# An audio block with experts on one core: TensorE signals per group instead of per matmul

## The chip, the cores and the metric

The kernel runs on one core of a Trainium2 chip. The metric is the device time of one execution in microseconds. A core has TensorE (matmuls and transposes), VectorE, ScalarE, GpSimd and SyncE, each with its own instruction stream; they wait for each other by semaphores, which an instruction raises when it is done. TensorE has a granted clock with two levels, 1.2 and 2.4 GHz.

## The reference

`x` is 64 x 125 x 128. Three steps, the second and third on a layernorm and added to their input:

```
conv = conv1d(x, kernel, window 3)                 # -> 64 x 123 x 384, cut in Z, F, O
c_t  = sigmoid(F) * c_{t-1} + (1 - sigmoid(F)) * tanh(Z);   h = sigmoid(O) * c_t
h    = h + gelu(long_conv(layernorm(h), filters from A, B) + h0 * layernorm(h))
logits = layernorm(h) @ gate.T;  top 2 of 16 experts per token;  weights = softmax(top values)
hid  = silu(x @ w1[e].T)                            # 512 wide, for each token's experts
mean = (sum of hid over the tokens of e) / count;   y[e] = mean @ w2[e].T
h    = h + weights[k] * y[expert k of the token], summed over k
```

So the experts need only the sum of `silu(x @ w1[e].T)` over the tokens routed to each expert.

## The kernel before, in words

The whole program is written out by hand, one function per engine; the order in each is the order of the calls there. Its parts in time: the recurrence over 16 chunks (to 127 us), the long convolution as Toeplitz matmuls (133 to 160), layernorm and logits, then the routing (178 to 244), the expert stage (248 to 403), the sums and the mix (to the end).

**Routing.** It goes in four parts of 16 sequences (`q` = 0 to 3, the first `QA` = 2 of them make a first list of tiles). For each part: `ranks` counts, `places` (VectorE) takes the place of each token in its expert's list, `bit_transposes` and `matches` make 16 of the 32 one-hot matrices on TensorE, four matmuls into two PSUM banks in turn, each read by one ScalarE activation (`low_onehots`, line 1164); VectorE makes the other 16. `picks` is 32 small matmuls, each with a signal on `pick_mm`; ScalarE copies their result (`copy_V`, line 1151), and `pick_transposes` turns it. The lists of token indices that result are what GpSimd gathers by.

**Expert stage.** `NT` = 138 tiles of 128 tokens, each tile for one expert. GpSimd gathers a tile from a table in HBM (line 586); the first 48 tiles have places of their own, the others go through a ring of 12 (four groups of three). Tiles stand in 45 groups of three and three groups of one. TensorE, for each group `g`: transposes of group `g + 1` into one bank (line 872), then the three experts of group `g` (line 898, 128 x 512, fp32, two matmul records a tile), each into one of six banks. ScalarE copies the transposed group to one of two buffers (line 1202) and does the Silu of each tile in place (line 1210). VectorE adds the bank to the sum of that tile's expert (line 1612). Which expert a tile has is read from SBUF into registers, six tiles at a time, by a load in TensorE's and in VectorE's stream (lines 888 and 1604), ahead of tiles 6, 12, 18 and so on. After tiles 23 and 26 TensorE also turns the routing weights (line 974), which VectorE makes between tiles 15 and 18 (lines 1688 and 1690), ScalarE copies (line 1238) and VectorE splits (line 1697). Tiles 0 to 47 are written out, 48 to 131 are a loop of twelve, the last six are written out.

The waits there: TensorE's transposes of group `g` wait for their gathers and for the copy of group `g - 1`; tile `n` waits for the addition of tile `n - 6`. ScalarE's copy of group `g` waits for its transposes and for the experts of group `g - 2`; the Silu of tile `n` waits for that tile (`expert_mm`). GpSimd gathers ring group `g` when the transposes of group `g - 4` are done (the first one that waits is group 20, for group 16).

Of the kernel before, what the change touches and what calls it, by code (L numbers as in the profile page):

```python
# [40 lines left out]
QB = 16  # L41
# [80 lines left out]
def build(nc, x, wconv, fa, fb, h0, gate, w1, w2, dft, idft, route, match, out, kpad, table):  # L122
# [11 lines left out]
    with ctx:  # L134
# [244 lines left out]
        g_transposed = sem("g_transposed")  # L379
        GT_ready = sem("GT_ready")  # L380
        expert_mm = sem("expert_mm")
# [47 lines left out]
        def _(sp):  # L429
# [77 lines left out]
            sp.wait_ge(g_transposed, EARLY_GROUPS)  # L507
# [8 lines left out]
        def _(pool):  # L516
# [97 lines left out]
        def _(pe):  # L614
# [113 lines left out]
            def picks(q):  # L728

                pe.wait_ge(OHc_ready, q + 1)  # L730
                for n in range(2 * QB):
                    if n >= ON_ACT:
                        pe.wait_ge(onehot, q * ((2 * QB - ON_ACT) // OB) + (n - ON_ACT) // OB + 1)
                    else:
                        pe.wait_ge(ring_read, MATCH_AT[q, n // OG] + 1)
                    b, k = n // 2, n % 2
                    nc.tensor.matmul(P[q][:, QW + b * E:QW + (b + 1) * E], ohl[q % 2][0:T, n],
                                     OHc[0:T, q % 2, k * QW + b * E:k * QW + (b + 1) * E], start=(k == 0),
                                     stop=(k == 1)).then_inc(pick_mm, 1)
# [7 lines left out]
            def matches(q):  # L747
                pe.wait_ge(bitsT_ready, q + 1)
                for a in range(PER_Q):
                    at = MATCH_AT[q, a]  # L750
                    pe.wait_ge(ring_read, at - 1)
                    part = slice(a * OG * BITS, (a + 1) * OG * BITS)
                    nc.tensor.matmul(PR[at % 2][0:T, :], bitsT[part, :], matchb[part, :],  # L753
                                     start=True, stop=True).then_inc(ring_mm, 1)
# [111 lines left out]
            def g_transposes(g, landed, sources):  # L866
# [6 lines left out]
                mm.then_inc(g_transposed, 1)  # L873
# [16 lines left out]
            def expert(n, bank, stat, k):  # L890
# [5 lines left out]
                elif n == 5:  # L896
                    pe.wait_ge(idx_ready, 2)
                nc.tensor.matmul(bank[:, :], stat, w1T[:, bass.ds(e * FF, FF)],  # L898
                                 start=True, stop=True).then_inc(expert_mm, 1)

            def expert_of(n):
# [8 lines left out]
                expert(n, expert_bank(n), GTs[:, g % 2, j * SLOT:(j + 1) * SLOT], n)  # L910
# [66 lines left out]
            with pe.Fori(UNROLLED // UNROLL, NT // UNROLL) as i:  # L977
                for j in range(UNROLL // GG):
# [7 lines left out]
                    for k in range(GG):  # L986
                        expert(i * UNROLL + j * GG + k, XP[(j * GG + k) % len(XP)],
                               GTs[:, j % 2, k * SLOT:(k + 1) * SLOT], j * GG + k)
# [46 lines left out]
        def _(act):  # L1035
# [102 lines left out]
            def code_OH(q):  # L1138
# [3 lines left out]
                if q >= 2:  # L1142
                    act.wait_ge(pick_mm, 2 * QB * (q - 1))
# [3 lines left out]
            def copy_V(q):  # L1147
                act.wait_ge(pick_mm, 2 * QB * (q + 1))
# [10 lines left out]
            def low_onehots(q):  # L1159
                for a in range(PER_Q):  # L1160
                    act.wait_ge(ring_mm, MATCH_AT[q, a] + 1)
                    if q >= 2:
                        act.wait_ge(pick_mm, 2 * QB * (q - 2) + (a + 1) * OG)
# [33 lines left out]
            def copy_GT(g, bank, done, count=GG):  # L1197

                act.wait_ge(g_transposed, g + 1)
                if done is not None:  # L1200
                    act.wait_ge(expert_mm, done)
                nc.scalar.copy(GTs[:, bank, 0:count * SLOT], PT[:, 0:count * SLOT]).then_inc(GT_ready, 1)  # L1202

            def copy_of(g):
                if g < len(GROUPS):
                    copy_GT(g, g % 2, sum(GROUPS[g - 2]) if g >= 2 else None, GROUPS[g][1])

            def silu(n, bank):
                act.wait_ge(expert_mm, n + 1)
                nc.scalar.activation(bank[:, :], bank[:, :], ACT.Silu).then_inc(silu_done, 1)  # L1210

            def silu_of(n):
                silu(n, expert_bank(n))
# [17 lines left out]
            for n in range(UNROLLED):  # L1231
                if n % GG == 0:
                    copy_of(n // GG + 1)
                silu_of(n)
                if n in RT_AT:
                    h = RT_AT.index(n)
                    act.wait_ge(RT_mm, h + 1)
                    nc.scalar.copy(xh[:, h, 0:4 * T], PRT[:, 0:4 * T]).then_inc(RT_high, 1)
            with act.Fori(UNROLLED // UNROLL, NT // UNROLL) as i:
                for j in range(UNROLL // GG):  # L1240
                    g = i * (UNROLL // GG) + j
                    copy_GT(g + 1, (j + 1) % 2, i * UNROLL + j * GG)
                    for k in range(GG):
                        silu(i * UNROLL + j * GG + k, XP[(j * GG + k) % len(XP)])
            for n in range(NT // UNROLL * UNROLL, NT):
                g = next(i for i, (first, count) in enumerate(GROUPS) if first <= n < first + count)
                if n == GROUPS[g][0]:
                    copy_of(g + 1)
                silu_of(n)
# [18 lines left out]
        def _(dve):  # L1268
# [235 lines left out]
            def low_onehots(q, part):  # L1504
                n = slice(ON_ACT + part * OB, ON_ACT + (part + 1) * OB)
                if q >= 2:
                    dve.wait_ge(pick_mm, 2 * QB * (q - 2) + n.stop)
# [176 lines left out]
            dve.wait_ge(pick_mm, 2 * QB * NQ)  # L1684
# [69 lines left out]
```

## Time and profile before

| | us |
|---|---|
| three runs | 440.21, 441.03, 1307.98 (median 441.03) |
| the profiled execution | 439.4 |
| its span (first to last instruction) | 437.7 |
| busy: TensorE, VectorE, ScalarE, GpSimd | 383.6, 312.4, 224.2, 208.0 |
| expert stage (first tile to last addition) | 248 to 403 |
| mean granted clock of TensorE | 0.927 of 2.4 GHz |

A row of a timeline gives the start, the duration, the engine, the line, what is written from what, and how many instructions are merged (x6 is three expert tiles). In brackets stands the time for which the engine was idle before, and what is taken to have ended it; this is the semaphore event that came last, and not always the one that the engine waited for. `PEld` is the weight load, `PEldq` TensorE's sequencer. The rows that the prediction uses stand in a section of their own below.

### The profile page before, as it was taken

What the parts mean: (1) busy time and instruction counts of PE and PEld (TensorE: products, weight loads), DVE (VectorE), ACT (ScalarE), POOL (GpSimd) and SP (SyncE); (2) the same over time, 40 slices, a digit from 0 to 9 for tenths busy, and PEclk for the clock granted to TensorE, in tenths of its full rate; (3) what the DMA queues carried; (4) which work ended last, traced back from release to release, by engine and by line L of the source; (5) the groups of instructions that cost most, each with busy time, mean ns of one, the idle gap of its engine ahead of it and who ended that gap; (6) DMA issues with size and microseconds to landing.
All of it is one profiled execution on the core that took longest, in us unless ns stands there. A gap on an engine that the chain in (4) does not pass through costs nothing.

```text
span 437.7 us, 6947 instructions
## 1 busy us (share of the span) xinstructions
PE 383.6 (88%) x1927; PEld 264.9 (61%) x1928; DVE 312.4 (71%) x829; ACT 224.2 (51%) x415; POOL 208.0 (48%) x229
## 2 busy tenths in 40 slices
PE   8999999999939989987765699899999978789983
PEld 7888888888739979855532344354444434345462
DVE  3498878887875879876757467766666665646993
ACT  3333555546422335764664277677666655556210
POOL 2002111110150007998677778726777777770700
PEclk9999999999979999985756599999999999999997
DMA  6301834241213085331964121219321112210059
GB/s 169 116 1 38 221 103 136 72 117 55 83 48 92 1 231 156 94 92 25 365 179 136 54 54 45 52 28 354 120 54 54 48 54 54 54 48 12 2 129 240
DMA packets 53016, 43.63 MB, mean 100 GB/s; under 512 B 20686, under 2 KB 45980, under 8 KB 52732
## 3 DMA queue, kind: packets, MB, share of 16 engines
q1 hardware_dynamic: 44276, 32.09, 25.0%
q0 software_dynamic: 4416, 9.05, 7.5%
q10 hardware_dynamic: 4296, 2.15, 1.8%
q8 instruction: 13, 0.21, 0.2%
q14 instruction: 15, 0.12, 0.1%
HBM read 34.86 MB, written 8.42 MB: 99 GB/s over the span
## 4 chain that ended last, share of the span: by engine, by line
PE 49%; issue 29%; DVE 11%; ACT 5%; POOL 3%; DVEq 1%; POOLq 0%; ACTq 0%
PE P L898 26%; PE P L834 6%; DVE BIG L1612 3%; PE P L872 3%; PE P L671 3%; DVE H L1728 3%; POOL rs L542 2%; PE P L1003 2%; PE P L663 2%; PE P L753 1%; PE P L680 1%; PE P L646 1%; ACT P L1210 1%; DVE arena L1586 1%; PE P L710 1%
## 5 line engine op out<-in xcount | busy, mean ns | idle before, releaser
L898 PE MATMUL P<-w1T,arena 128*128 x276 | 129.8, 606 | 12.9 <-DVE BIG L1612 8.0
L1612 DVE TENSOR_TENSOR BIG<-BIG,P 128x512 f32 x138 | 95.0, 688 | 58.9 <-ACT P L1210 43.2
L1210 ACT ACTIVATE P<-P 128x512 f32<-128x512 f32 x138 | 80.3, 582 | 53.3 <-PE P L898 53.3
L586 POOL DMA_INDIRECT arena<-table,arena x90 | 85.1, 946 | 35.8 <-issue 26.5
L898 PEld LDWEIGHTS P<-w1T,arena 128*128 128x128 f32 x276 | 48.7, 192 | 62.7 <-issue 62.1
L542 POOL TENSOR_TENSOR rs<-ve,mhalf 123x4 f32<-123x4 f32 x16 | 17.9, 1118 | 106.1 <-DVE ve L1282 106.1
L586 POOL DMA_INDIRECT XN<-table,arena x48 | 49.8, 1038 | 17.2 <-issue 14.3
L1044 ACT ACTIVATE arena<-P 128x492 f32<-128x492 f32 x48 | 27.9, 583 | 50.2 <-PE P L628 50.1
L628 PE MATMUL P<-xh,wh 128*128 128x498 f32 x144 | 41.9, 399 | 0.0
L628 PE MATMUL P<-xh,wl 128*128 128x498 f32 x144 | 40.5, 390 | 0.0
L628 PE MATMUL P<-xl,wh 128*128 128x498 f32 x144 | 40.4, 389 | 0.0
L628 PEld LDWEIGHTS P<-xl,wh 128*128 128x128 f32 x144 | 27.2, 189 | 5.6
L628 PEld LDWEIGHTS P<-xh,wl 128*128 128x128 f32 x144 | 27.1, 188 | 5.4
L570 POOL TENSOR_TENSOR arena<-arena,mhalf 123x16 f32<-123x16 f32 x4 | 11.9, 2966 | 35.2 <-DVE arena L1429 35.2
L628 PEld LDWEIGHTS P<-xh,wh 128*128 128x128 f32 x144 | 25.8, 189 | 4.1
L573 POOL TENSOR_SCALAR XN<-H,arena 123x128 f32<-123x128 f32 x32 | 27.5, 872 | 0.4
L834 PE MATMUL P<-XN,BIG 123*123 123x112 f32 (+1 forms) x256 | 27.6, 271 | 0.0
L834 PEld LDWEIGHTS P<-XN,BIG 123*123 123x123 f32 x256 | 27.6, 188 | 0.0
L1202 ACT COPY arena<-P 128x384 f32<-128x384 f32 (+1 forms) x48 | 22.6, 472 | 1.2 <-PE P L872 1.1
L1287 DVE SCALAR_TENSOR_TENSOR arena<-arena 128x492 f32<-128x492 f32 x16 | 10.7, 670 | 17.2 <-ACT arena L1044 17.2
L1408 DVE TENSOR_TENSOR H<-H,arena 123x512 f32<-123x512 f32 x16 | 20.2, 1279 | 3.8 <-ACT arena L1120 3.8
L872 PEld LDWEIGHTS P<-ident,arena 128*128 128x128 f32 x90 | 11.3, 141 | 17.7 <-issue 17.7
(235 smaller groups left out, 605.0 us busy)
## 6 DMA issues: line engine op xcount, KB each, us to landing
arena<-kpad SPq DMA_DIRECT2D x16, 492.0 KB, 4.1
XN<-in_L_ffn_w SPq DMA_DIRECT2D x1, 4096.0 KB, 15.4
arena<-in_x SPq DMA_DIRECT2D x16, 224.0 KB
table<-XN SPq DMA_DIRECT2D x4, 896.0 KB
BIG<-table SPq DMA_DIRECT2D x1, 2048.0 KB, 7.4
out<-H SPq DMA_DIRECT2D x8, 224.0 KB
out<-H ACTq DMA_DIRECT2D x8, 224.0 KB
arena<-table,arena POOLq DMA_INDIRECT x90, 2.5
```

The source lines that it names most:

```text
L542: nc.gpsimd.tensor_tensor(rs1[0:T, k], ve1[0:T, k], mhalf[0:T, 0:CB], ALU.pow).then_inc(rstd1, 1)
L573: a = nc.gpsimd.tensor_scalar(XN[0:T, b], H[0:T, b], mm2[0:T, 0, b:b + 1], rs2[0:T, b:b + 1], ALU.subtract, ALU.mult)
L586: pool.indirect_dma_start(out=row_of(n), out_offset=None, in_=table[0:(QA * QB + 1) * TROW, :] if n < NA else table[:, :], in_offset=bass. ...
L628: mm = nc.tensor.matmul(PG[g][:, 0:NV], wpart[:, w, g * D:(g + 1) * D], xpart[:, k, w:w + NV], start=(place == 0 and w == 0), stop=(place ...
L834: mm = nc.tensor.matmul(PG[g % 3][0:T, j * B:j * B + n], hank[0:T, c // HP % HRES, c % HP], XF[0:T, c * B:c * B + n], start=True, stop=True)
L872: mm = nc.tensor.transpose(PT[:, j * SLOT:(j + 1) * SLOT], src, ident[:])
L898: nc.tensor.matmul(bank[:, :], stat, w1T[:, bass.ds(e * FF, FF)], start=True, stop=True).then_inc(expert_mm, 1)
L1044: nc.scalar.activation(dst[:, k].rearrange("p (b t) -> p b t", b=CB), src, func).then_inc(gate_act, 1)
L1202: nc.scalar.copy(GTs[:, bank, 0:count * SLOT], PT[:, 0:count * SLOT]).then_inc(GT_ready, 1)
L1210: nc.scalar.activation(bank[:, :], bank[:, :], ACT.Silu).then_inc(silu_done, 1)
L1408: v.tensor_tensor(hv, hv, gl[0:T, g % 2], ALU.add).then_inc(H_added, 1)
L1612: v.tensor_tensor(at, at, bank[:, :], ALU.add).then_inc(esum_step, 1)
```

## The change

TensorE gives fewer signals. `g_transposed` and `expert_mm` are gone, and one semaphore `group_mm` takes their place: the transposes of group 0 raise it, and then the first expert tile of every group. That tile stands behind the transposes of the next group and behind the last tiles of the group before it, so its signal tells that all of these are done. `pick_mm` is raised once per part, by the last of 32 picks. In the last two parts of the routing the matches signal in pairs.

```diff
@@ picks
...
-                                     stop=(k == 1)).then_inc(pick_mm, 1)
...
+                                          stop=(k == 1))
+                mm.then_inc(pick_mm, 1)
@@ matches
-                                     start=True, stop=True).then_inc(ring_mm, 1)
+                                          start=True, stop=True)
+                    if q < QA:
+                        mm.then_inc(ring_mm, 1)
+                    elif a % 2 == 1:
+                        mm.then_inc(ring_mm, 2)
@@ g_transposes
-                mm.then_inc(g_transposed, 1)
+                if isinstance(g, int) and g == 0:
+                    mm.then_inc(group_mm, 1)
@@ expert (opens is true for the first tile of a group)
-                                 start=True, stop=True).then_inc(expert_mm, 1)
+                                      start=True, stop=True)
+                if opens:
+
+                    mm.then_inc(group_mm, 1)
@@ GpSimd, gathers of the ring
-                    pool.wait_ge(g_transposed, g - (GSLOTS if g >= EARLY_GROUPS + GSLOTS else EARLY_GROUPS) + 1)
+                    pool.wait_ge(group_mm, g - (GSLOTS if g >= EARLY_GROUPS + GSLOTS else EARLY_GROUPS) + 1)
@@ ScalarE, copy_V
-                act.wait_ge(pick_mm, 2 * QB * (q + 1))
+                act.wait_ge(pick_mm, q + 1)
@@ ScalarE, expert stage
-                act.wait_ge(g_transposed, g + 1)
-                if done is not None:
-                    act.wait_ge(expert_mm, done)
+                act.wait_ge(group_mm, g + 1)
...
-            def silu(n, bank):
-                act.wait_ge(expert_mm, n + 1)
+                else:
+                    act.wait_ge(group_mm, g + 1)
+
+            def silu(bank):
...
+            def silus_past(g):
+
+                copy_of(g + 1)
+                for n in range(GROUPS[g - 1][0] + 1 if g else 0, GROUPS[g][0] + 1):
+                    silu_of(n)
+                    if n in RT_AT:
+                        h = RT_AT.index(n)
+                        act.wait_ge(RT_mm, h + 1)
+                        nc.scalar.copy(xh[:, h, 0:4 * T], PRT[:, 0:4 * T]).then_inc(RT_high, 1)
```

TensorE's, VectorE's and GpSimd's streams hold the same instructions in the same order as before. ScalarE's has other waits and, in the written-out part, other groups of Silus. Its start of the expert stage before (L1202 is the copy of a transposed group, L1210 the Silu; `x3` are three tiles):

```order
L1202 COPY arena<-P 128x384 [waits g_transposed] x2
L1210 ACT_TABLE_LOAD
L1210 ACTIVATE P<-P 128x512 [waits expert_mm] x3
L1202 COPY arena<-P 128x384 [waits expert_mm,g_transposed]
L1210 ACTIVATE P<-P 128x512 [waits expert_mm] x3
```

The same place now (L1209 is the copy, L1218 the Silu):

```order
L1209 COPY arena<-P 128x384 [waits group_mm] x2
L1218 ACT_TABLE_LOAD
L1218 ACTIVATE P<-P 128x512
L1209 COPY arena<-P 128x384 [waits group_mm]
L1218 ACTIVATE P<-P 128x512 x3
L1209 COPY arena<-P 128x384 [waits group_mm]
```

Copy 2 stood behind the Silu of tile 2 and now stands behind that of tile 0; the Silus of tiles 1, 2 and 3 stand behind it, without a wait. The last tiles on ScalarE before (groups of one tile):

```order
L1202 COPY arena<-P 128x128 [waits expert_mm,g_transposed]
L1210 ACTIVATE P<-P 128x512 [waits expert_mm] x3
L1202 COPY arena<-P 128x128 [waits expert_mm,g_transposed]
L1210 ACTIVATE P<-P 128x512 [waits expert_mm]
L1202 COPY arena<-P 128x128 [waits expert_mm,g_transposed]
L1210 ACTIVATE P<-P 128x512 [waits expert_mm] x2
```

And now:

```order
L1209 COPY arena<-P 128x128 [waits group_mm]
L1218 ACTIVATE P<-P 128x512 x3
L1209 COPY arena<-P 128x128 [waits group_mm]
L1218 ACTIVATE P<-P 128x512 x3
L1209 COPY arena<-P 128x128 [waits group_mm]
L1218 ACTIVATE P<-P 128x512
L1218 ACTIVATE P<-P 128x512 [waits group_mm]
L1262 CAST oner<-onef 128x128
```

Each copy there waits for the tile of the group before it, and the Silus of tiles 133 to 135 stand behind the copy that waits for tile 135.

## Rows read from the trace of the kernel before

**Rows 1.** TensorE in order of time: start, duration, what, [idle before it, who ended that].

```profile
255.41 2.74 PE L898 MATMUL P<-w1T,arena 128*128 x6
...
258.32 2.74 PE L898 MATMUL P<-w1T,arena 128*128 x6
260.90 0.49 PE L872 MATMUL P<-ident,XN 128*128 128x128 f32 x3
...
274.70 2.84 PE L898 MATMUL P<-w1T,arena 128*128 x6 [0.87 <-ACT arena L1202]
278.64 0.61 PE L974 MATMUL P<-ident,arena 123*128 123x123 f32 x4 [1.11 <-DVE xl L1697]
```

**Rows 2.** Stretches: busy time of the engines (PE, PEld, DVE, ACT, POOL), TensorE clock, DMA.

```profile
247.90:272.90 25.00, 25.00 (x70) 11.63 (x70) 15.90 (x22) 17.14 (x31) 19.44 (x19) 0.93 0.19 51
...
345.00:393.00 48.00, 39.48 (x114) 17.94 (x115) 28.56 (x42) 27.39 (x52) 36.41 (x39) 1.00 0.19 53
```

**Rows 3.** GpSimd in order of time: the first and the last of 78 gathers.

```profile
297.29 0.95 POOL L586 DMA_INDIRECT arena<-table,arena  x1 [8.66 <-PE P L872]
...
393.61 0.94 POOL L586 DMA_INDIRECT arena<-table,arena  x1 [0.30 <-issue]
```

**Rows 4.** TensorE in order of time, 285 to 438 us.

```profile
296.52 0.49 PE L872 MATMUL P<-ident,arena 128*128 128x128 f32 x3
...
366.36 0.54 PE L872 MATMUL P<-ident,arena 128*128 128x128 f32 x3
368.22 2.84 PE L898 MATMUL P<-w1T,arena 128*128 x6 [1.32 <-DVE BIG L1612]
...
398.93 1.02 PE L898 MATMUL P<-w1T,arena 128*128 x2
...
400.14 1.98 PE L898 MATMUL P<-w1T,arena 128*128 x4
```

**Rows 5.** VectorE's last addition, from all engines in order of time.

```profile
402.92 0.69 DVE L1612 TENSOR_TENSOR BIG<-BIG,P 128x512 f32 x1 [0.21 <-ACT P L1210]
```

**Rows 6.** All engines in order of time, 196.5 to 206 us.

```profile
197.10 1.05 PE L737 MATMUL P<-arena 123*128 123x16 bf16 x32
...
198.44 0.37 ACT L1151 COPY arena<-P 128x256 f32<-128x256 f32 x1 [0.51 <-PE P L737]
```

**Rows 7.** All engines in order of time, 217 to 248.5 us.

```profile
222.39 1.26 PE L753 MATMUL P<-matchb,arena 32*123 32x512 bf16 x2 [0.78 <-ACT arena L1164]
...
223.11 1.27 ACT L1164 ACTIVATE arena<-P,below 123x512 bf16<-123x512 f32 x2 [0.19 <-PE P L753]
...
224.43 0.70 PE L737 MATMUL P<-arena 123*128 123x16 bf16 x20 [0.31 <-ACT arena L1164]
```

**Rows 8.** ScalarE in order of time, 248 to 300 us.

```profile
252.88 0.49 ACT L1202 COPY arena<-P 128x384 f32<-128x384 f32 x1
...
254.43 0.58 ACT L1210 ACTIVATE P<-P 128x512 f32<-128x512 f32 x1 [0.28 <-PE P L898]
...
256.48 0.58 ACT L1210 ACTIVATE P<-P 128x512 f32<-128x512 f32 x1 [0.21 <-PE P L898]
...
272.96 0.58 ACT L1210 ACTIVATE P<-P 128x512 f32<-128x512 f32 x1 [0.44 <-PE P L898]
273.53 0.57 ACT L1238 CAST xh<-P 128x492 fp32r<-128x492 f32 x1
```

**Rows 9.** TensorE's register load of line 888: count, ns (least/median/most), start.

```profile
L888 PEldq TENSOR_LOAD <-arena x1: 1475/1475/1475, 253.5 to 253.5; - x1
```

**Rows 10.** VectorE in order of time, 248 to 283 us.

```profile
256.09 0.69 DVE L1612 TENSOR_TENSOR BIG<-BIG,P 128x512 f32 x1 [0.21 <-DVE BIG L1612]
257.81 0.69 DVE L1612 TENSOR_TENSOR BIG<-BIG,P 128x512 f32 x1 [1.03 <-ACT P L1210]
...
271.58 1.22 DVE L1690 TENSOR_TENSOR arena<-arena 123x1024 f32<-123x1024 f32 x1
```

**Rows 11.** The chain that ended last: start, duration, what.

```profile
277.23 0.69 DVE BIG L1612
```

More of the change, by code:

```diff
@@ L506, in _ @@
                 write_table(g)
-            sp.wait_ge(g_transposed, EARLY_GROUPS)
+            sp.wait_ge(group_mm, EARLY_GROUPS)
             sp.dma_start(w2_sb, w2.rearrange("e d f -> d e f")).then_inc(w2_in, 16)
@@ L752, in matches @@
                     part = slice(a * OG * BITS, (a + 1) * OG * BITS)
-                    nc.tensor.matmul(PR[at % 2][0:T, :], bitsT[part, :], matchb[part, :],
-                                     start=True, stop=True).then_inc(ring_mm, 1)
+                    mm = nc.tensor.matmul(PR[at % 2][0:T, :], bitsT[part, :], matchb[part, :],
+                                          start=True, stop=True)
[3 more added lines that the diff above has]
+                        mm.then_inc(ring_mm, 2)
             def pick_transposes(q):
@@ L888, in load_experts, with expert @@
                 pe.load(regs[block % 2], eid[0:1, bass.ds(at, REGS)])
-            def expert(n, bank, stat, k):
+            def expert(n, bank, stat, k, opens):
                 e = pe.snap(regs[k // REGS % 2][k % REGS], min_val=0, max_val=E - 1)
@@ L897, in expert @@
                     pe.wait_ge(idx_ready, 2)
-                nc.tensor.matmul(bank[:, :], stat, w1T[:, bass.ds(e * FF, FF)],
-                                 start=True, stop=True).then_inc(expert_mm, 1)
+                mm = nc.tensor.matmul(bank[:, :], stat, w1T[:, bass.ds(e * FF, FF)],
+                                      start=True, stop=True)
+                if opens:
+                    mm.then_inc(group_mm, 1)
             def expert_of(n):
@@ L909, in expert_of @@
                 j = n - GROUPS[g][0]
-                expert(n, expert_bank(n), GTs[:, g % 2, j * SLOT:(j + 1) * SLOT], n)
+                expert(n, expert_bank(n), GTs[:, g % 2, j * SLOT:(j + 1) * SLOT], n, j == 0)
             for q in range(3):
@@ L1195, in _, with copy_GT @@
                 copy_w1T(m)
-            def copy_GT(g, bank, done, count=GG):
-                act.wait_ge(g_transposed, g + 1)
-                if done is not None:
-                    act.wait_ge(expert_mm, done)
+            def copy_GT(g, bank, count=GG):
+                act.wait_ge(group_mm, g + 1)
                 nc.scalar.copy(GTs[:, bank, 0:count * SLOT], PT[:, 0:count * SLOT]).then_inc(GT_ready, 1)
@@ L1230, in _ @@
             copy_of(0)
[L1231 to L1238, printed above, removed]
+            for g in range(UNROLLED // GG):
+                silus_past(g)
             with act.Fori(UNROLLED // UNROLL, NT // UNROLL) as i:
@@ L1241, in _ @@
                     g = i * (UNROLL // GG) + j
[L1242 to L1249, printed above, removed]
+                    copy_GT(g + 1, (j + 1) % 2)
+                    for k in range(1 - GG, 1):
+                        silu(XP[(j * GG + k) % len(XP)])
+            for g in range(NT // UNROLL * UNROLL // GG, len(GROUPS)):
+                silus_past(g)
             nc.scalar.copy(oner[:], onef[:])
```

23 lines of the change are left out of this document (11 added, 12 removed).

## The prediction

> **What bounds the kernel now.** I read the timelines first, because the change touches one long stage, the 138 expert tiles from 248 to 403 us, and the routing just ahead of it. In the timeline of TensorE the reader is to see a regular pattern: three tiles in 2.58 us (0.86 each), then the three transposes of the next group, and the next tiles 2.90 us after the last ones [rows 1]. Nothing stands between two tiles, and this although each of them gives a signal: TensorE is full in the first 25 us of the stage [rows 2]. From 345 to 393 us it is busy for 39.5 of 48 us; there GpSimd sets the pace. Its ring of twelve gathered tiles begins with a gather at 297.29 us, after 8.66 us of waiting for TensorE's transposes of group 16, and from there 78 gathers follow without a pause, the last at 393.61, one every 1.25 us [rows 3]. Three such gathers are 3.75 us, against TensorE's 2.90. So the stage has two parts. Until the transposes of group 16 (296.52 us, [rows 4]) every delay of TensorE moves the ring. After it, only what moves the ring, or comes behind its last gather, counts. The stage ends with VectorE's last addition, at 402.92 us [rows 5], and what follows is the same in both kernels.
>
> **What the change can save.** A signal taken off a matmul is worth what TensorE or its reader lose by it. In the expert stage the rows leave nothing for TensorE: three tiles start 0.86 us apart with signals. I cost this edit at nothing. For the picks, 32 matmuls take 1.05 us and ScalarE's copy begins at 198.44, 0.29 us after their end [rows 6]. If all 32 signals stood in this gap, three such gaps on the path (the fourth is behind VectorE) give 0.9 us; if none did, nothing. I take 0.4 us.
> Here a rule speaks for the change. The Trainium skill ("TensorE: Matmul & The Clock Gate", section "The cost: per-tile semaphore tail") says that signals of matmuls are written one after another, 26.3 ns each. By that rule 31 signals fewer would give 0.8 us at each burst, if they all queued up. The trace doesn't agree, since the whole gap is 0.29 us.
>
> **The match pairs.** In the last two parts of the routing, ScalarE's third one-hot activation now waits for the fourth match too, and that one waits for the bank that the second activation reads. In the third part the matches 3 and 4 run from 222.39 to 223.65, and activation 3 begins at 223.11 [rows 7]; it would begin at about 223.7. The picks behind it, at 224.43, wait for activation 4, and behind them stand the ranks of the last part: +0.6 us on the path. In the fourth part the picks wait for VectorE's one-hots anyway (without that cover it would be 0.6 more). Of the first pair the second match costs nothing that I count. Routing: +0.6 - 0.4 = **+0.2 us**.
>
> **The register load.** Before every sixth tile TensorE's sequencer loads six expert numbers, behind the wait of the next transposes for ScalarE's last copy. For tile 6 this copy ran from 252.88 to 253.37 [rows 8], and the load began at 253.5 and took 1.47 us [rows 9]. A tile behind a load that isn't hidden starts 1.86 us after its transposes, 366.36 to 368.22 [rows 4], so about 1.75 after the copy's end. Tile 6 could have started at 255.2, and started at 255.41 [rows 1]: hidden, with 0.2 us to spare. Now the copy needs the signal of tile 3 rather than that of the transposes ahead of it. ScalarE answers a tile 1.07 us after the tile's start (255.41 to 256.48, [rows 1, 8]); tile 3 starts 2.90 before tile 6, so the copy begins at 253.58 rather than 252.88, 0.7 us later. Of this 0.45 to 0.5 is not hidden, and I take 0.45. It comes back at tiles 6, 12, 18, 30, 36 and 42 ahead of the ring: 6 x 0.45 = **+2.7 us**. Ends: nothing, if the sequencer finds other slack, and 0.65 each.
>
> **The additions come later.** Before, each Silu ran right behind its tile: that of tile 4 at 254.43 [rows 8]. Now it waits for tile 6, which starts at 255.86, for the signal (1.07) and for the copy (0.45): 257.4, so 3.0 us later. Silus behind it need no wait and follow every 0.5 to 0.57 us (272.96 to 273.53, [rows 8]). VectorE needs 0.90 us an addition and 1.72 at a load (256.09 to 257.81, [rows 10]), 6.2 us for six tiles; TensorE will need 5.8 + 0.45. So VectorE doesn't catch up, and stays 3.0 us behind its old times. The six banks take that, until the routing weights: VectorE's sum at line 1690 ends at 272.80 [rows 10], TensorE turns it round behind tile 23, and tile 24 came at 274.70 [rows 1]. Three us later is 277.7, of which 1.35 were counted at tiles 6, 12, 18: **+1.6 us** more. Before the second turn TensorE waited 1.11 us for line 1697 [rows 1], behind the additions of the chain at 277.23 [rows 11]; tile 23 is now held for tile 24's signal, which gives **+0.5**. Ends for both together: nothing and 3 us. Transposes of group 16: 2.7 + 1.6 + 0.5 = +4.8 us.
>
> **The ring.** GpSimd was let go by the transposes of group 16, 0.77 us after their start (296.52 to 297.29, [rows 3, 4]). Now it is let go by the first tile behind them, which starts 0.32 later and answers after 1.0: 1.35 us after their start. **+0.6 us.** All 78 gathers follow and carry the shift on; the releases behind this one have slack, because GpSimd needs 3.75 us a group.
>
> **The end.** The last three groups hold one tile each, so their signals come in a chain: the transposes of tile 137 wait for a copy that waits for tile 135, and tile 137 waits for a copy that waits for tile 136. Before, tile 135 started at 398.93, tile 136 at 400.14 and tile 137 0.86 behind it [rows 4]. Now, counted from tile 135 at t: copy at t + 1.1, transposes at t + 1.6, tile 136 at t + 1.75, its copy at t + 2.8, tile 137 at t + 3.55. Meanwhile VectorE gets tiles 133 to 135 together after t + 1.5 and needs 0.90 each. Tile 135 is 5.5 late (404.4), tile 137 starts at 408.0, and the last addition comes at about 410.7, where it was 402.92: 7.8 us, of which 5.4 came with the ring. **+2.4 us**, between 1.5 and 3.
>
> **Sum**: 0.2 + 4.8 + 0.6 + 2.4 = 8.0 us. The profiled execution took 439.4 us (span 437.7), which gives 447.4. The runs of 440.21 and 441.03 (the median) are 0.8 and 1.6 above it, so I put the median at **448.2 us**, 1.6% over 441.03. About 2% (8.8 us) is what a measurement of this kernel tells from no change.
>
> **Rivals.**
> 1. *Faster: signals do hold TensorE up.* For it: picks come in dense bursts, and a burst may last as long as its signals do. Then three bursts of 1.05 us and their gaps of 0.29 [rows 6] could shrink by at most 4 us, and 3 of these with nothing lost elsewhere give 438. Against: tiles in the stage stand back to back. Chance 0.07.
> 2. *Slower by over 2%: the clock falls.* TensorE will stand for some 2 us before tile 24 and again before tile 27, where it stood for about 1 us each. In the first 25 us of the stage the mean granted clock was 0.93 [rows 2], which is 3.5 us at 1.2 GHz and costs 1.8. One such spell near 277 us gives 448.2 + 1.8 = 450, two give 451.8. It decides if the clock of that stretch falls below 1.00. Chance 0.15.
> 3. *The load stays hidden.* If the sequencer gets past the transposes' wait, the 2.7 us go, and with them some of the lag: 444.5 to 445.5. Against: the load began 0.1 us after the copy ended [rows 8, 9]. Chance 0.18.
> 4. *The lateness stays off the path.* Fewer waits on ScalarE and six banks absorb the batches, only the ring's 0.6 is left: 441.5. Against: line 1690 is on TensorE's path. Chance 0.07.
> My forecast has 0.53.
>
> **Numbers.** The range from 443.0 to 451.0 takes in the bounds of the load (-2.7, +1.2), of the lag (-2.1, +0.9) and of the end, most of rivals 2 and 3, and leaves out rivals 1 and 4 and two falls of the clock. Slower by over 2% (above 449.9): rival 2 and the upper edge of my forecast, 0.23. Faster by over 2%: 0.02; the signals can't be worth 9 us. Within 2%: 0.75.
>
> **What would show it.** Right: tile 6 starts 3.3 to 3.4 us after tile 3, and so at every load; Silus come in threes behind a copy; tile 24 starts about 3 us later than now; the ring's first gather comes near 303 us and 78 follow at 1.25; tiles 136 and 137 stand nearly 2 us apart. Wrong: six tiles still in 5.81 us before the ring, additions of tiles 16 to 23 at their old distance from their tiles, TensorE's picks shorter than 1.05 us, or gaps between GpSimd's gathers after the first of the ring.

## The result and the profile after

The changed kernel took 449.94 us (median of four runs, 448.31 to 451.21), the kernel before 440.62 us beside it (median of four runs; one of them, 1307.98, was disturbed, and without it the median is 440.21). The ratio is 1.022, 95% interval 1.0195 to 1.0241: 9.3 to 9.7 us slower. The forecast was 448.2 us, the range 443.0 to 451.0. The profiled execution took 448.31 us with a span of 446.6 us, 8.9 us more than before.

The page of the kernel after, first the busy time of the engines, then the clock line of the 40 slices, the shares of the chain that ended last, and the two groups of instructions that changed most:

```profile
PE 386.8 (87%) x1927; PEld 265.8 (60%) x1928; DVE 312.1 (70%) x829; ACT 214.8 (48%) x415; POOL 207.8 (47%) x229
...
PEclk9999999999969989965865799999999999999998
...
PE 41%; issue 31%; DVE 14%; ACT 6%; DVEq 3%; POOL 3%; POOLq 0%; ACTq 0%
...
L904 PE MATMUL P<-w1T,arena 128*128 x276 | 130.8, 608 | 17.2 <-DVE BIG L1622 11.7
L1622 DVE TENSOR_TENSOR BIG<-BIG,P 128x512 f32 x138 | 95.0, 688 | 67.5 <-ACT P L1218 45.0
```

The reader is to see that the work is the same: VectorE is as busy as before, ScalarE 9 us less (three Silus in a row overlap in this count, their mean is unchanged), TensorE 3.2 us more with the same 1927 matmuls, 1.0 of it in the expert tiles. The rest of the time went into waits. TensorE's share of the final chain fell from 49% to 41%, VectorE's rose from 11% to 14%.

TensorE in order of time, at the first register load that matters (answers to [rows 1]):

```profile
252.81 2.74 PE L904 MATMUL P<-w1T,arena 128*128 x6
...
256.24 2.84 PE L904 MATMUL P<-w1T,arena 128*128 x6 [0.36 <-issue]
...
259.24 2.74 PE L904 MATMUL P<-w1T,arena 128*128 x6
```

Tile 6 starts 3.43 us after tile 3, where it was 2.90, and tile 9 3.00 after tile 6, where it was 2.91: the load of six expert numbers now shows as a wait for "issue", and it costs 0.6 us for six tiles, the 0.1 at the group behind it counted in. ScalarE at the same time (answers to [rows 8]):

```profile
253.87 0.48 ACT L1209 COPY arena<-P 128x384 f32<-128x384 f32 x1 [1.04 <-PE P L904]
...
257.40 0.48 ACT L1209 COPY arena<-P 128x384 f32<-128x384 f32 x1 [1.58 <-PE P L904]
257.77 1.57 ACT L1218 ACTIVATE P<-P 128x512 f32<-128x512 f32 x3
```

The copy is 1.0 us later than before (0.7 of it against the start of tile 3) and waits for an expert tile (L904), and the Silus come three at a time behind it. The Silu of tile 4 was at 254.43 and is now the first of the batch at 257.77.

VectorE, then TensorE, where the routing weights are turned (answer to [rows 10] and [rows 1]):

```profile
275.09 1.22 DVE L1700 TENSOR_TENSOR arena<-arena 123x1024 f32<-123x1024 f32 x1
```

```profile
275.31 1.12 PE L904 MATMUL P<-w1T,arena 128*128 x2 [1.00 <-DVE BIG L1622]
276.36 0.64 PE L983 MATMUL P<-ident,arena 123*128 123x123 f32 x4
...
278.21 2.84 PE L904 MATMUL P<-w1T,arena 128*128 x6 [0.87 <-DVE BIG L1622]
282.79 0.61 PE L983 MATMUL P<-ident,arena 123*128 123x123 f32 x4 [1.74 <-DVE xl L1707]
```

VectorE's sum (L1690 before, L1700 now) starts at 275.09 instead of 271.58. TensorE waits 1.00 us for a bank at tile 23, which it did not before, tile 24 comes at 278.21 instead of 274.70, and the second turn waits 1.74 us instead of 1.11.

GpSimd (answers to [rows 3]) and TensorE's transposes that let it go (to [rows 4]), each in order of time:

```profile
304.15 0.94 POOL L585 DMA_INDIRECT arena<-table,arena  x1 [15.79 <-PE P L904]
...
400.28 0.94 POOL L585 DMA_INDIRECT arena<-table,arena  x1 [0.30 <-issue]
```

```profile
302.53 0.49 PE L877 MATMUL P<-ident,arena 128*128 128x128 f32 x3
302.86 2.74 PE L904 MATMUL P<-w1T,arena 128*128 x6
```

The transposes of group 16 are 6.01 us late and the ring 6.86. From there 78 gathers follow again, one every 1.25 us, the last 6.67 us later than before: the ring carries the shift and adds nothing.

The end. First TensorE, then VectorE (answer to [rows 4, 5]):

```profile
405.86 1.02 PE L904 MATMUL P<-w1T,arena 128*128 x2
407.33 0.30 PE L877 MATMUL P<-ident,arena 128*128 128x128 f32 x1 [0.45 <-ACT arena L1209]
407.55 1.12 PE L904 MATMUL P<-w1T,arena 128*128 x2
409.20 1.12 PE L904 MATMUL P<-w1T,arena 128*128 x2 [0.54 <-DVE BIG L1622]
```

```profile
402.16 0.69 DVE L1622 TENSOR_TENSOR BIG<-BIG,P 128x512 f32 x1 [1.16 <-ACT P L1218]
403.06 0.69 DVE L1622 TENSOR_TENSOR BIG<-BIG,P 128x512 f32 x1 [0.21 <-DVE BIG L1622]
...
412.06 0.69 DVE L1622 TENSOR_TENSOR BIG<-BIG,P 128x512 f32 x1 [0.21 <-DVE BIG L1622]
```

Tiles 135, 136 and 137 stand 1.69 and 1.65 us apart, as the chain of signals wanted. But the last addition is set by VectorE itself: from 402.16 it does twelve additions in a row at 0.90 us, 402.16 + 11 x 0.90 = 412.06. It came late to the end and had no pause left in which to catch up. Both stand close together here: the Silu of tile 137 starts at 410.36, and 0.76 us behind it, as before, VectorE could have added at 411.12, had it been free.

### The profile page after: what moved, and what is told of

Same layout as the page of the kernel before. It is cut to its first block, busy times and chain, and to the rows that moved or that the text cites. A ratio compares the mean times of both kernels' runs of the same rounds, so it can differ in the third digit from the quotient of the medians.

```text
span 446.6 us, 6815 instructions
## 1 busy us (share of the span) xinstructions
PE 386.8 (87%) x1927; PEld 265.8 (60%) x1928; DVE 312.1 (70%) x829; ACT 214.8 (48%) x415; POOL 207.8 (47%) x229
## 4 chain that ended last, share of the span: by engine, by line
PE 41%; issue 31%; DVE 14%; ACT 6%; DVEq 3%; POOL 3%; POOLq 0%; ACTq 0%
PE P L904 19%; PE P L839 6%; DVE BIG L1622 6%; ACT P L1218 3%; PE P L670 3%; DVE H L1738 2%; DVEq L1614 2%; PE P L877 2%; POOL rs L541 2%; PE P L1012 2%; PE P L662 2%; PE P L754 1%; PE P L679 1%; PE P L645 1%; DVE arena L1596 1%
## 5 line engine op out<-in xcount | busy, mean ns | idle before, releaser
L904 PE MATMUL P<-w1T,arena 128*128 x276 | 130.8, 608 | 17.2 <-DVE BIG L1622 11.7
L585 POOL DMA_INDIRECT arena<-table,arena x90 | 87.7, 974 | 42.9 <-issue 24.4
L904 PEld LDWEIGHTS P<-w1T,arena 128*128 128x128 f32 x276 | 48.8, 192 | 69.1 <-issue 68.5
L1218 ACT ACTIVATE P<-P 128x512 f32<-128x512 f32 x138 | 72.7, 581 | 0.9 <-PE P L904 0.9
L1209 ACT COPY arena<-P 128x384 f32<-128x384 f32 (+1 forms) x48 | 22.3, 464 | 71.7 <-PE P L904 71.7
L585 POOL DMA_INDIRECT XN<-table,arena x48 | 47.1, 982 | 16.7 <-issue 14.3
```

Source lines behind the costliest of these rows:

```text
L585: pool.indirect_dma_start(out=row_of(n), out_offset=None, in_=table[0:(QA * QB + 1) * TROW, :] if n < NA else table[:, :], in_offset=bass. ...
L904: mm = nc.tensor.matmul(bank[:, :], stat, w1T[:, bass.ds(e * FF, FF)], start=True, stop=True)
```

## The experiments

Nine kernels ran in twelve experiments, on three chips. a_load, a_copy, a_release and b_picks_load ran on a chip on which the kernel before took what it takes in the main result (440.14 us, 13 runs). On the two other chips, A (b_picks, b_pairs, b_group, a_unread) and B (a_three and the names that end in 2), the kernel before itself took 511.55 and 512.29 us. The traces from there have long waits ahead of and inside the expert stage, put down to "remote" (20 and more in each of the eight, none in the six others); their times spread by some 10 us, and from them I take mainly what a trace shows in stretches without such waits. To compare the profiles of these first four kernels with the two main ones I use one origin in all, the start of TensorE's transposes of group 1 (246.17 us before, 246.66 after). Shifts against the kernel before, in us, worked out from the timelines (before: 50.35, 51.12, 147.44 and 157.57 us behind the origin; the last column is the matmul of line 1003 behind the last additions):

| kernel | time, ratio to before [95%] | transposes of group 16 | ring's first gather | last gather | line 1003 |
|---|---|---|---|---|---|
| the change | 449.94, 1.022 [1.0195, 1.0241] | +5.52 | +6.37 | +6.18 | +8.58 |
| a_load | 445.32, 1.0115 [1.0085, 1.0145] | +3.23 | +4.08 | +4.07 | +5.07 |
| a_copy | 446.74, 1.0154 [1.0123, 1.0186] | +2.19 | +3.04 | +2.84 | +5.07 |
| a_release | 448.91, 1.0198 [1.0169, 1.0228] | +5.81 | +5.80 | +5.62 | +8.03 |
| b_picks_load | 438.57, 0.9964 [0.9946, 0.9981] | -0.46 | -0.46 | -0.68 | -1.33 |

**a_load: the register load ahead of the transposes.** The theory says that the load is exposed because it stands behind the transposes' wait for a later copy. Here it is issued before that wait.

```diff
                 if n % GG == 0:
+                    load_before(n)
                     transposes_of(n // GG + 1)
                 expert_of(n)
```

> The changed kernel, with TensorE's register load moved ahead of the transposes (and so of their wait for ScalarE's copy and for the gathers); every signal and wait as in the changed kernel. Theory: tile 6 starts 2.9 us after tile 3, tile 12 2.9 to 3.2 after tile 9; transposes of group 16 1.7 us sooner or more; in the ring's half the 1.3 us gaps at every sixth tile go but the pace stays at GpSimd's 1.25 us a gather; time 3 us (0.7%) below the changed kernel, 1.3 of it behind the last gathers. Rival (the load isn't what stands before tile 6): no change.

TensorE of this kernel in order of time:

```profile
254.74 2.74 PE L904 MATMUL P<-w1T,arena 128*128 x6
...
257.64 2.74 PE L904 MATMUL P<-w1T,arena 128*128 x6
...
269.42 0.52 PE L877 MATMUL P<-ident,XN 128*128 128x128 f32 x3 [0.22 <-issue]
...
279.18 0.52 PE L877 MATMUL P<-ident,XN 128*128 128x128 f32 x3 [1.00 <-issue]
```

Tiles 3, 6 and 9 start 2.90 us apart again. The load isn't hidden everywhere, though: at tiles 18 and 24 the transposes behind it now wait for it, 0.22 and 1.00 us, and at tile 42 0.24 (this load runs from 297.9 for 1.46 us, the transposes start at 299.56). The transposes of group 16 come 2.3 us sooner than in the changed kernel, the median is 4.6 us lower. Another 1.4 us comes at the end: between the last gather and line 1003 a_load has 1.0 (5.07 - 4.07) over the kernel before, and the changed kernel 2.4. Some of this the kernel before could have had too, since it has exposed loads in the ring ([rows 4], tile at 368.22); b_picks_load, below, gains 0.65 there. Against that kernel a_load still has 1.7 at the end, so of the 2.4 that the change loses there 0.7 is the load's. That the median fell by more than the trace's 3.5 us is within what single profiles differ by.

**a_copy: the copy waits for the transposes again.** The transposes behind those of group 0 get a semaphore of their own, and ScalarE's copy waits for that; the Silus stay in batches behind the first tile of the next group.

```diff
+                else:
+                    mm.then_inc(later_t, 1)
...
-                act.wait_ge(group_mm, g + 1)
+                    act.wait_ge(later_t, g)
                 nc.scalar.copy(GTs[:, bank, 0:count * SLOT], PT[:, 0:count * SLOT]).then_inc(GT_ready, 1)
...
                 copy_of(g + 1)
+                act.wait_ge(group_mm, g + 2)
```

> The changed kernel, but the transposes signal again and ScalarE copies a transposed group on that signal; the Silus still come in threes on the group signal, and GpSimd's ring too. Theory: TensorE's register load is hidden again, tile 6 starts 2.9 us after tile 3 rather than 3.43, at every load; the additions stay late, so tile 24 still comes 1.5 to 2 us later than in before; transposes of group 16 come 3.1 us sooner, time 3.5 us (0.8%) below the changed kernel. Rival (the load costs only because additions are late): no change at tiles 6, 12 and 18, under 1 us in the time.

```profile
253.11 2.74 PE L907 MATMUL P<-w1T,arena 128*128 x6
...
256.01 2.74 PE L907 MATMUL P<-w1T,arena 128*128 x6
...
274.40 1.12 PE L907 MATMUL P<-w1T,arena 128*128 x2 [1.00 <-DVE BIG L1628]
275.45 0.64 PE L986 MATMUL P<-ident,arena 123*128 123x123 f32 x4
277.31 2.84 PE L907 MATMUL P<-w1T,arena 128*128 x6 [0.88 <-ACT arena L1215]
281.50 0.61 PE L986 MATMUL P<-ident,arena 123*128 123x123 f32 x4 [1.36 <-DVE xl L1713]
```

With the load where it was and only the copy early, tile 6 starts 2.90 us after tile 3: it was the copy's lateness that exposed the load. The shift of group 16 falls from 5.52 to 2.19, so the loads were worth 3.3 us. The median is 3.2 us below the changed kernel's, as expected. a_load, which moves the load and leaves the copy late, keeps 1.0 us more of the shift (3.23), since its load still stands in front of some transposes. What is left is the wait of tile 23, the late tile 24 and the second turn, that is, the batches of Silus. The end keeps its cost: from the last gather to line 1003 it is +2.2 over before, with copies that no longer wait for a tile. Its VectorE, in order of time, adds without a pause up to the end here too:

```profile
399.01 0.69 DVE L1628 TENSOR_TENSOR BIG<-BIG,P 128x512 f32 x1 [1.15 <-issue]
...
408.91 0.69 DVE L1628 TENSOR_TENSOR BIG<-BIG,P 128x512 f32 x1 [0.21 <-DVE BIG L1628]
```

**a_release: GpSimd is let go by the transposes again.**

```diff
-                    pool.wait_ge(group_mm, g - (GSLOTS if g >= EARLY_GROUPS + GSLOTS else EARLY_GROUPS) + 1)
+                    behind = g - (GSLOTS if g >= EARLY_GROUPS + GSLOTS else EARLY_GROUPS)
+                    if behind == 0:
+                        pool.wait_ge(group_mm, 1)
+                    else:
+                        pool.wait_ge(later_t, behind)
```

> The changed kernel, but the transposes of the later groups signal again and GpSimd's ring waits for them; all else waits for the group signal. Theory: only the ring's release moves: the first gather of the ring comes 0.85 us sooner after the transposes of group 16 (0.77 instead of 1.62), these stay where they are, and the time is 0.85 us (0.2%) below the changed kernel. Rival (ring releases further on bind too): more than 1.5 us below.

The ring's first gather starts 0.76 us after the transposes of group 16, as before (0.77), where the changed kernel has 1.62. The shift grows by nothing at this place (+5.81, +5.80). The time is 1.0 us below the changed kernel's, where 0.85 was expected, with the two intervals overlapping; the place and the size are shown by the trace, the gain in the time only roughly.

**b_picks_load: what is worth keeping.** The kernel before, with one signal for the 32 picks and the load ahead of the transposes, and nothing of the expert stage's edit.

```diff
-                                     stop=(k == 1)).then_inc(pick_mm, 1)
+                                          stop=(k == 1))
+                mm.then_inc(pick_mm, 1)
...
                 if n % GG == 0:
+                    load_before(n)
                     transposes_of(n // GG + 1)
```

> The kernel before with one signal for the picks of a part and with TensorE's register load ahead of the transposes: what the theory would keep. Theory: 0.5 us from the picks, nothing ahead of the ring since the load is hidden there, 0.6 to 1 us behind the last gathers: 1.1 to 1.5 us (0.3%) below before. Rival: the load ahead of the transposes delays them and costs 1 us or more.

438.57 us against 440.14: 1.6 us faster, and the interval leaves out no change. The trace has 1.3 us of it behind the origin: 0.46 at the first tiles, which no longer wait for a load behind the transposes, 0.22 up to the last gather and 0.65 behind it. From the groups by line, the expert matmuls (columns as in the page: busy, mean ns, idle before):

```profile
L899 PE MATMUL P<-w1T,arena 128*128 x276 | 129.3, 605 | 0.0
L873 PE MATMUL P<-ident,arena 128*128 128x128 f32 x90 | 15.9, 282 | 10.3 <-DMA arena<-table,arena 7.4 <-issue 2.8
```

The expert tiles of the kernel before had 12.9 us of waits and its transposes of the ring 0.1. These waits have mostly moved from the tiles to the transposes, which wait for gathers and for the load, and not gone: in the ring GpSimd sets the pace either way. What the picks' signals give lies ahead of the origin and can't be told there from the 0.8 us by which the two origins differ. This is the version that beats both kernels, by little.

**The edits one by one, on chip A.** The kernel before with one edit each: the picks, the matches, the expert stage. The edits are those of the diff above; b_group keeps one signal for each pick and each match. The edit of the picks also moves the other waits on `pick_mm`: the one-hots of a part wait for all picks of the part two before, where they waited for their own share of them.

> The kernel before with one signal for the 32 picks of a part, nothing else changed. Theory (signals cost TensorE nothing; only the gap from the last pick to ScalarE's copy shrinks, 0.29 to 0.04 us after a full burst, less after a short one): a part's burst keeps its 1.05 us, three gaps on the path give 0.4 to 0.75 us, the time is 0.1 to 0.2% below before. Rival (signals pace the burst): 32 picks take clearly less than 1.05 us and the time falls by 2 to 4 us.

> The kernel before with the matches of the last two parts signalling in pairs, nothing else changed. Theory: in the third part the third one-hot activation begins 0.6 us later after the first, the first pair costs 0.1 us, and the ranks of the last part 0.7 us later; the fourth part's pair is hidden, except for 0.1 of its first pair at most. The first expert tile and the end come 0.7 us later (+0.15%). Rival (the picks wait for VectorE there too): no change of the first tile's start.

> The change's third part alone: one signal per group of three tiles in the expert stage, picks and matches as before. Theory (this part is the whole loss): first tile at the old 247.9 us, transposes of group 16 about 5.6 us after those of before, first gather of the ring 6.4 us later, last addition 8.6 us later, time 8.5 us (1.9%) above before. Rival (much of the loss is in the routing): under 7 us above before.

| kernel | us (before 511.55) | ratio [95%] |
|---|---|---|
| b_picks | 512.25 | 1.0030 [0.9999, 1.0060] |
| b_pairs | 512.88 | 1.0047 [1.0003, 1.0092] |
| b_group | 517.32 | 1.0136 [1.0083, 1.0189] |

**Two of them again, on chip B.**

> The kernel before with the edit of the matches alone (one signal for two matches in the last two parts of the routing). Theory: the picks of the third part and the ranks behind them come 0.5 to 0.7 us later, so the first expert tile and the time too: +0.5 to +0.7 us, ratio 1.001 to 1.002. Rival (the picks of that part wait for something else): no difference.

> The kernel before with the expert stage's edit alone (one signal for three tiles; picks and matches signal as before). Theory: nearly all of the loss is here, ratio 1.018 to 1.021 against before (+8 to +9 us), transposes of group 16 some 5.6 us later, ring +6.5, end +2.2. Rival (the edits in the routing carry a part of the loss): 1.015 or less.

b_pairs2 took 510.82 us (before: 512.29), ratio 0.9961 [0.9923, 0.9998], b_group2 517.32 us, 1.0119 [1.0080, 1.0158]. The two results of the pairs exclude each other by a hair, so on these chips such an interval is too narrow by some us, and their cost is too small for these times to show. The expert stage's edit has a loss both times, 7.0 and 6.1 us by the ratios (5.8 and 5.0 between the medians), while neither edit of the routing has a loss that repeats. That is less than the 8 to 9 us that I expected, and by its number b_group2 meets its rival (1.015 or less), b_group stands at the edge of its own. But the rival's reason, a part of the loss in the routing, isn't what the kernels with the routing's edits show. The whole change did not run on chips A and B, so that the expert stage's edit is nearly all of the loss rests on the main profiles: the first tile is 0.45 us late there, the last addition 9.14. On chips A and B part of a delay may vanish in the "remote" waits; that is not shown. In a stretch without such waits the two kernels with the edit agree: from the transposes of group 8 to those of group 16 b_group2 takes 30.75 us, and the changed kernel in the main profile 30.78. Without the edit it is 26.1 in b_pairs2 and 26.8 in the kernel before.

The pairs are visible in the third part of the routing of b_pairs2 against b_picks, but ScalarE's copy behind them then waits 17.7 us in both, put down to "remote". The picks for which the code makes it wait had ended by 239.2 and it ran at 256.15 (b_pairs2), and only GpSimd's gathers run in between; what held it is open. In the main profile they stand on the path. TensorE and ScalarE after, third part (answers to [rows 7]):

```profile
222.25 1.32 PE L754 MATMUL P<-matchb,arena 32*123 32x512 bf16 x2 [0.84 <-ACT arena L1173]
...
223.60 1.26 ACT L1173 ACTIVATE arena<-P,below 123x512 bf16<-123x512 f32 x2 [0.83 <-PE P L754]
...
224.92 0.70 PE L736 MATMUL P<-arena 123*128 123x16 bf16 x20 [0.30 <-ACT arena L1173]
```

The third activation waits 0.83 us where it waited 0.19, and starts at 223.60 instead of 223.11; the picks follow at 224.92 instead of 224.43.

**a_unread and a_unread2: the signals as before, nobody reads them.** The changed kernel, in which all the picks, transposed groups and expert tiles that lost their signal raise a semaphore that no engine waits for (the matches stay in pairs). The same kernel ran twice.

```diff
                 if opens:
 
                     mm.then_inc(group_mm, 1)
+                else:
+                    mm.then_inc(unread[1], 1)
...
                 if isinstance(g, int) and g == 0:
                     mm.then_inc(group_mm, 1)
+                else:
+                    mm.then_inc(unread[0], 1)
...
                                           stop=(k == 1))
+                    if n < 2 * QB - 1:
+                        mm.then_inc(unread[2], 1)
                 mm.then_inc(pick_mm, 1)
```

> The changed kernel, with a signal again on every expert tile, every transposed group and every pick, on semaphores that nobody waits for. Theory (it is the waits that moved, not the signals): the same time as the changed kernel within 0.1%, expert tiles 0.86 us apart, and the gap from the last pick to ScalarE's copy either stays 0.04 us (then the other waits of the copy mattered) or returns to 0.29 (then signals do stand in a row), which moves the time by at most 0.75 us. Rival (signals cost TensorE time that the change saved): slower than the changed kernel by 2 us or more.

> The changed kernel, where every pick and every expert tile signals again, but to semaphores that nobody waits for: TensorE writes as many signals as before, and the waits are those of the change. Theory (a signal that nobody reads costs TensorE nothing in the expert stage, and at a burst of picks the 0.25 us by which the signal behind it comes later): within 0.9 us of the changed kernel, slower if anything, expert tiles 0.86 us apart. Rival (signals hold TensorE up, at 26.3 ns each as one reads the page on TensorE of the Trainium skill, or more): 3 x 0.8 us and more for the picks, over 2 us slower than the changed kernel.

The first burst of picks and ScalarE's copy behind it, from all engines in order of time: a_unread2, and then the kernel after (answers to [rows 6]).

```profile
197.13 1.05 PE L737 MATMUL P<-arena 123*128 123x16 bf16 x32
...
198.47 0.37 ACT L1167 COPY arena<-P 128x256 f32<-128x256 f32 x1 [0.51 <-PE P L737]
```

```profile
197.22 1.05 PE L736 MATMUL P<-arena 123*128 123x16 bf16 x32
...
198.31 0.37 ACT L1160 COPY arena<-P 128x256 f32<-128x256 f32 x1 [0.26 <-PE P L736]
```

The burst takes 1.05 us with 32 signals and with one. The copy starts 0.29 us behind it with them and 0.04 without: 31 signals ahead of the last one delay it by 0.25 us. In the expert stage the signals cost nothing: from the transposes of group 8 to those of group 16 a_unread2 takes 30.75 us, just as b_group2. The times (515.65 us, ratio 1.0109 [1.0063, 1.0155], and 519.10 us, the median of four runs from 513.31 to 522.39, 1.0162 [1.0102, 1.0222]) lie on both sides of b_group's 1.0136 and 1.0119 and are too wide to settle 1 us; the changed kernel itself did not run beside them, so it is the trace that answers, not the time. By the rule of the Trainium skill that the prediction cites ("TensorE: Matmul & The Clock Gate", section "The cost: per-tile semaphore tail"), 26.3 ns for a signal, the delay of the copy would be 0.8 us; here it is 8 ns a signal.

**a_three: all three repairs, the Silus still in batches.** The edits of a_load, a_copy and a_release together.

> The changed kernel with three repairs at once: a signal of its own for the transposes behind those of group 0, which lets ScalarE's copy and GpSimd's ring go, and the register load ahead of the transposes. What is left of the change is that each Silu batch waits for the first tile of the next group. Theory (terms add, the additions' lateness is a cost of its own): against the kernel before +0.45 routing, no load stalls, tile 24 and 27 together 2 to 2.4 us late, ring release 0.77 us behind the transposes as before, end +1 to +1.5 us; against the changed kernel -5 to -6.5 us, so 443.5 to 445 us, 0.8 to 1.1% over before. Rival (the lateness of the additions costs only because the load and the copy stand behind it): nothing of it left, 440 to 441 us, no difference from before.

511.95 us against 512.29 for the kernel before, ratio 1.0023 [0.9985, 1.0061]: by the ratio 1.2 us slower, between -0.8 and +3.1, by the medians 0.3 faster. That is less than I expected, and the time doesn't exclude the rival. The trace does. TensorE of a_three in order of time:

```profile
317.25 0.49 PE L882 MATMUL P<-ident,XN 128*128 128x128 f32 x3
...
320.42 1.12 PE L911 MATMUL P<-w1T,arena 128*128 x2 [0.96 <-DVE BIG L1634]
321.48 0.64 PE L992 MATMUL P<-ident,arena 123*128 123x123 f32 x4
323.11 0.52 PE L882 MATMUL P<-ident,XN 128*128 128x128 f32 x3 [0.99 <-issue]
```

With no late copy and no load in front of it, TensorE still waits 0.96 us for a bank at tile 23, and the turn of the weights starts 4.23 us after the transposes of group 8, where it is 2.90 in b_pairs2. The 0.99 us behind the turn is the moved load itself (it runs from 321.5 for 1.46 us); tile 24's bank came free at 322.94, so it costs little. From the transposes of group 8 to those of group 16 it takes 28.4 us, against 26.1 in b_pairs2 (which has none of this) and 30.75 in b_group2: the late copy and load are 2.3 us of this stretch, the late additions about 2, and some tenths are what still shows of the moved load. The end also stays: 8.9 us from the transposes of group 45 to the last addition, against 7.15 in b_pairs2 and 9.33 in b_group2. I had put the end lower because I took the chain of copies for its cause.

## Why the prediction was right, point by point

| step | predicted | measured | from |
|---|---|---|---|
| routing | +0.2 | +0.3 to 0.45 | first tile 248.35, before 247.90; tile 3 252.81, before 252.51 |
| register loads up to group 16 | +2.7 | +3.3 to 3.6 | 0.5 at each of six and 0.1 at the group behind; a_copy |
| late additions, tiles 24 and 27 | +2.1 | +2.1 to 2.2 | 1.45 and 0.63 in the main profiles; a_copy; a_three |
| release of the ring | +0.6 | +0.85 | 1.62 and 0.77; a_release |
| end | +2.4 | +2.2 to 2.4 | line 1003 at 412.81, before 403.74 |
| sum | +8.0 | +9.1 | last addition +9.14; span +8.9, medians +9.3 |

The mechanism and the places were right. The loads make most of the difference, 0.6 to 0.9 us of 1.1; the routing and the ring came out slightly larger too, the late additions and the end at their size, the end partly by luck.

- *Nothing for signals in the expert stage, 0.4 us for the picks.* Right in kind. The gap behind the first burst shrank by 0.25 us, those behind the second and third by 0.14 each (0.18 to 0.04), 0.53 in all; the time of the picks' edit alone could not be told from zero.
- *The pairs.* Predicted +0.6. The third part's picks and the ranks behind them are 0.49 and 0.35 us later, although the gain of the picks in the first part lies ahead of them. The second match of the first pair, which I counted as nothing, costs 0.13 us. The fourth part's pairs were not hidden either: the first transpose of its bits comes 0.32 us late, the small matmuls behind its matches (line 951 before, 960 now) 0.51 and its picks 0.51, so 0.2 is added there, since VectorE's one-hots wait behind those matmuls. I also left out that the profiles differ by up to 2.3 us ahead of the expert stage (the origin at 246.66 in the changed kernel, 248.92 in a_load) where their code is the same.
- *The load.* I took 0.45 from a range of 0 to 0.65. The wait shows 0.52 to 0.53, with 0.1 more at the group behind it, which I did not count: this term was mis-sized, 0.6 where I had 0.45. That the copy's lateness exposes it is shown by a_copy, which leaves the load alone. I left out that loads are exposed in the kernel before too, ahead of tile 0 and in the ring; a_load and b_picks_load found it.
- *The lag.* VectorE's sum came 3.51 us later than before, and so did tile 24. I had 3.0 with the loads' delay in it, and the routing's 0.2. The banks did not take it all: tile 23 waited 1.00 us. That wait cost nothing more, since the turn of the weights behind it waited for the same VectorE.
- *The ring.* Right in kind, 0.25 us short: GpSimd starts 1.29 us after the first tile's start, not 1.03. The 78 gathers moved as one.
- *The end.* Right in size, wrong in its cause. I derived it from the chain of signals of the three single tiles and gave VectorE 0.90 us an addition in passing. The chain is there (1.69 and 1.65 us), but a_copy and a_three, whose copies don't wait for tiles, keep 2.2 and 1.8 us of it, and by a_load 0.7 us of the end belongs to the load, which I had not put there. That the size came out is luck. What holds is that VectorE enters the end a batch late and adds twelve tiles back to back.
- *Rivals.* The clock did not fall: in the stretch where TensorE waits most it was granted in full, by the busy times of stretches of the kernel after (columns as in [rows 2]):

```profile
248.40:273.40 25.00, 23.85 (x66) 11.10 (x67) 13.19 (x19) 14.27 (x28) 19.15 (x20) 0.94 0.19 51
273.40:284.00 10.60, 6.99 (x26) 3.18 (x26) 7.94 (x11) 4.12 (x9) 8.47 (x8) 1.00 0.16 44
```

The result lies at 449.9, where I had put one fall of the clock (450), but it isn't one. The forecast was 1.7 us lower: 0.9 are the misses of the terms (the profiled execution took 448.31 us, forecast 447.4), and the rest is how far the median stands above the profiled execution, 1.6 us here where I had taken 0.8. Signals did not hold TensorE up (a_unread), the load did not stay hidden, and the lateness did not stay off the path. What stays open is the pairs' and the picks' share in the time, each below 1 us by the trace, and the expert stage's edit alone was not measured where the kernel before takes 440 us.

## What to carry to other kernels

A signal that is moved to a later instruction delays every reader by the distance between the two, and readers behind the reader too: look for what stands behind the wait, here a register load, a chain of additions and a ring of gathers. An engine with hardly any slack does not give a lateness back: ahead of the ring VectorE has 6.2 us of work for six tiles, TensorE took 5.8 for them and now takes 6.4, and VectorE is 3.3 us late at tile 6 and 3.5 at its sum. It is paid wherever another engine meets it. In the ring VectorE has pauses (1.2 to 1.5 us ahead of a batch), so there each batch is late anew, and the last one is paid at the end. Merge signals where the reader waits for the last one anyway, as with the 32 picks. Here that gained at most some tenths of a microsecond, while every merge that moved a signal to a later instruction cost time.

## What the runs showed of the hardware

- 32 signals in a row don't lengthen the burst of matmuls (1.05 us both ways); the reader of the last one starts 0.25 us later, 8 ns for each of the 31 others.
- A register load of six numbers takes 1.47 us of TensorE's sequencer (23 of them, median 1469 ns). It started only after the wait written ahead of it, so a copy 0.7 us later exposed 0.5 of it. Moved ahead of that wait it was mostly hidden, and where it wasn't the transposes waited for it (0.22 to 1.00 us in a_load).
- The same kernel took 440 us on one chip and 512 on two others. All eight traces from those two show waits of up to 10 to 19 us in the routing and, in the ring, pauses of mostly 2.2 us after every nine or ten gathers, both put down to "remote"; the six traces at 440 to 450 us have no wait of this name. What these waits are, and whether the chip is their cause, no run shows.
